# Swin block and convolution block over 16 images: the front of image n+2 made in the feed-forward stretch of image n+1

## The reference

```
t    = layernorm(tok)                                  # tok: 1024 tokens x 128, in 16 windows of 64
q, k, v = t @ qkv_w.T + qkv_b                          # 8 heads of 16
a    = softmax(q k^T / 4 + bias) v                     # in each window
tok  = tok + a @ proj_w.T + proj_b
tok  = tok + gelu(layernorm(tok) @ w1.T + b1) @ w2.T + b2     # 128 -> 512 -> 128

out0 = gelu(conv1x1(x));  x_att, adaptive = from the mean of out0
x_fca = |x_att| * |out0|                               # what abs(ifft2(fft2(out0) * x_att)) gives
x_sca = fgm(conv1x1(mean x_fca) * x_fca)               # fft2, high frequencies boosted, abs(ifft2)
h, v = 1x7 and 7x1 dilated, then 3x3, all depthwise;   pyr = four dilated 3x3 grouped, then 3x3
edge = sigmoid(conv3x3(out0)); cw = softmax(base * adaptive)
out  = conv1x1(relu(x + cw0 (1+edge) h + cw1 (1+edge) v + cw2 (1-.3 edge) pyr + cw3 point + cw4 x_sca))
```

## Time and profile before

| | us |
|---|---|
| runs shown: lowest, median, highest of 3 | 1802.71, 1813.92, 1819.46 |
| the profiled execution: its own time | 1805.41 |
| its span, first to last instruction | 1803.6 |
| from one `rectify` to the next, 15 cycles apart in all | 106.57 to 109.88 |

### The profile page before, as it was taken

One profiled execution on the slowest core, in us unless ns is written; L12 is line 12 of the kernel. 1 busy time (PEld: TensorE's weight loads), 2 busy tenths in 40 slices (PEclk: granted clock), 3 DMA queues, 4 the chain that ended last, 5 costly groups with the idle time before them and its releaser, 6 DMA issues.

```text
span 1803.6 us, 32142 instructions
## 1 busy us (share of the span) xinstructions
PE 1549.4 (86%) x11664; PEld 906.3 (50%) x11664; DVE 1364.0 (76%) x2455; ACT 864.2 (48%) x1380; POOL 684.9 (38%) x603
## 2 busy tenths in 40 slices
PE   5789899888989889888998988889888898988884
PEld 3346455464555546445463554546455464555542
DVE  4558778687777878788687777868788786778866
ACT  2344545455454544545455454544545545454533
POOL 3244251634416244251534416134251623416151
PEclk9899999999999999999999999999999999999997
DMA  4011020111102011020111102011020201102020
GB/s 147 1 26 41 26 52 1 43 33 37 39 23 53 0 37 39 25 51 0 43 33 37 39 23 53 0 37 39 25 51 0 58 18 37 39 12 53 0 54 12
DMA packets 19618, 60.23 MB, mean 33 GB/s; under 512 B 6228, under 2 KB 6228, under 8 KB 19204
## 3 DMA queue, kind: packets, MB, share of 16 engines
q1 hardware_dynamic: 19588, 59.83, 13.7%
HBM read 14.04 MB, written 9.02 MB: 13 GB/s over the span
## 4 chain that ended last, share of the span: by engine, by line
DVE 39%; PE 25%; DVEq 16%; issue 7%; ACT 6%; SPq 4%; DMA 3%; ACTq 1%; POOL 0%; POOLq 0%
DVE hv L1090 16%; DVEq L959 7%; DVE nT L929 5%; PE bank L647 5%; PE bank L674 4%; SPq L428 4%; DVE row_max L960 4%; DVEq L965 3%; PE bank L467 3%; PE bank L518 3%; PE bank L489 2%; DMA k_heads<-kC 2%; PE bank L755 2%; DVE score L957 2%; PE bank L577 1%
## 5 line engine op out<-in xcount | busy, mean ns | idle before, releaser
L674 PE MATMUL bank<-act,mats_sb 128*32 128x512 f32 (+11 forms) x2112 | 267.1, 475 | 1.4 <-DVE xs L1026 1.4
L1666 POOL TENSOR_TENSOR score<-score,row_max 128x512 f32<-128x512 f32 x128 | 133.4, 1042 | 306.7 <-DVE row_max L960 305.1
L1350 ACT ACTIVATE fft<-bank 128x512 f32<-128x512 f32 x224 | 168.9, 807 | 125.7 <-PE bank L467 111.8
L1090 DVE SCALAR_TENSOR_TENSOR hv<-hor,mix,hv 128x1024 f32<-128x1024 f32 x128 | 193.8, 1514 | 10.7
L467 PE MATMUL bank<-cons_sb,fft 128*128 128x128 f32 x1280 | 185.4, 306 | 11.8 <-DVE fft L1117 11.8
L1090 DVE SCALAR_TENSOR_TENSOR hv<-ver,mix,hv 128x1024 f32<-128x1024 f32 x144 | 186.9, 1298 | 11.0
L1382 ACT ACTIVATE score<-score 128x512 f32<-128x512 f32 x128 | 80.8, 631 | 225.8 <-POOL score L1666 225.8
L467 PEld LDWEIGHTS bank<-cons_sb,fft 128*128 128x128 f32 x1280 | 172.7, 217 | 31.4 <-DVE fft L1117 17.0
L1677 POOL COPY inv_wide<-row_inv 128x128 f32<-128x128 f32 x128 | 91.8, 717 | 206.7 <-DVE row_inv L966 206.7
L674 PEld LDWEIGHTS bank<-act,mats_sb 128*32 128x32 f32 x2112 | 117.5, 109 | 99.6 <-issue 81.5
L1696 POOL TENSOR_SCALAR hor<-act,cols_sb 128x1024 f32<-128x1024 f32 x16 | 18.0, 1125 | 391.6 <-ACT act L1407 391.6
(11 more groups left out here) (180 smaller groups left out, 2903.9 us busy)
## 6 DMA issues: line engine op xcount, KB each, us to landing
pyr_stack<-pyr SPq DMA_DIRECT2D x192, 144.2 KB, 3.1
x_in<-x_dram SPq DMA_DIRECT2D x16, 512.0 KB, 3.5
k_heads<-kC SPq DMA_DIRECT2D x128, 64.0 KB, 2.4
out_dram<-y_out SPq DMA_DIRECT2D x16, 512.0 KB, 2.8
k_heads<-rel_dram SPq DMA_DIRECT2D x2, 1024.0 KB, 13.0
mats_sb<-mats_dram SPq DMA_DIRECT2D x1, 1978.5 KB, 7.4
z_dram<-z_sb SPq DMA_DIRECT2D x32, 19.1 KB
z_run<-z_dram SPq DMA_DIRECT2D x16, 38.2 KB
```

What stands on the lines that cost most here:

```text
L674: last = pe.matmul(grids[32 * d:32 * d + 32, y0 - 16 * k:y1 - 16 * k, x0:x1], w_pyr[:, d, t], act[:, y0 + dy:y1 + dy, x0 + dx:x1 + dx], st ...
L1090: last = dve.scalar_tensor_tensor(hv[:], src, mix[:, a, k:k + 1], hv[:], ALU.mult, ALU.add)
L1350: return act_.activation(dst, src, ACT.Copy)
L1666: pool.tensor_tensor(score[:, j % 3], score[:, j % 3], row_max[:, j % 3].unsqueeze(2).broadcast_to([P, HEADS, WT]), ALU.subtract)\
```

## The change

The first steps of the Swin block, from the tokens to queries, keys and values (its *front*), leave the front of the cycle and go one cycle earlier. `both(n, i, f)` now has three images in work: the convolution block of n, attention and feed-forward of i = n+1, and the front of f = n+2. The last cycle has f = None. `swin_rest(0, 1)` makes the front of image 1 too, and the front of image 0 is made before it.

- The next image's token transposes go through bank 3 in slots 6 and 7 (`next_turns`), `norm1_stats(f)` after slot 7, `norm1(f)` after the fourteenth tap, and its n transposes, keys, queries and values between the up and down products of `mlp`, in banks 4 to 7, which the convolution block has emptied by then.
- New tiles: `attn_out` has its own memory (and holds nC1, the transposed first normalisation), `xT` shares memory with `qC`, `x1T` has its own, statistics of the two normalisations are apart.
- Waits: `in_conv` waits for the queries of the front (bank 4, 5), `gap_products`, `edge_products` and `out_conv` for its values (bank 6, 7), `spread_inverse(i, 1)` for `x_copy(f)` (bank 3).
- `SLOT_TAPS` goes from 9 to 13 taps in the slots. The second half of the pyramid, of which 5 of 9 steps stood ahead of slot 0, now lies wholly in slots 0 and 1, and its waits for `route_z` and `xs_sb` are gone. `conv_early` stands before `scores(i, j+2)`. `r_even_bias` stands before slot 3's taps.
- SP issues `spread_keys(n+2)` and `load(n+3)` behind `stack_pyramid(n)`.

```diff
-        attn_out = xw
-        xT = sb("xT", CH, C)
-        x1T = xT
+        attn_out = sb("attn_out", TOK)
+        nC1 = attn_out
+        x1T = sb("x1T", CH, C)
+        xT = qC.rearrange("p (c d) -> p c d", c=CH)
...
-        SLOT_TAPS = (0, 0, 0, 2, 4, 4, 5, 7, 9)
+        SLOT_TAPS = (0, 0, 0, 2, 4, 6, 7, 10, 13)
...
+            with sp.Fori(0, IMAGES - 3) as n:
                 spread_edge(n)
-                spread_keys(n + 1)
                 stack_pyramid(n)
+                load(n + 3)
+                spread_keys(n + 2)
                 store(n)
...
-            def mlp(i):
+            def mlp(i, n=None, f=None):
...
+                def value(k):
+                    pe.wait_ge(k_sb, 2 * f + k + 1)
+                    v(f, k, 6 + k)
                 for t in range(3):
-                    up(t)
+                    up(i, t)
                 n2_transposes(i, 1)
-                for t in range(3, 6):
-                    up(t)
-                down(0)
-                up(6)
-                up(7)
-                down(1)
+                up(i, 3)
+                up(i, 4)
+                half_of(turn, 0)
+                up(i, 5)
+                half_of(turn, 1)
+                down(i, 0)
+                half_of(key, 0)
+                half_of(key, 1)
+                up(i, 6)
+                half_of(query, 0)
+                half_of(query, 1)
+                up(i, 7)
+                half_of(value, 0)
+                half_of(value, 1)
+                down(i, 1)
...
+            def next_turns(i, f, k):
+                if k == 0:
+                    pe.wait_ge(s_biased, 8 * i + 8)
+                else:
+                    pe.wait_ge(xT_sb, 2 * f + 1)
+                x_transposes(f, k, 3)
...
             # PE
-            def both(n, i):
-                in_conv(n)
-                x_transposes(i)
+            def both(n, i, f):
+                scores(i, 0)
+                in_conv(n, i + 1)
+                scores(i, 1)
                 edge_products(n)
                 pyramid(n, 0, range(0, 2))
                 gap_products(n)
-                pyramid(n, 0, range(2, 7))
-                n_transposes(i)
+                pyramid(n, 0, range(2, 6))
                 mid_products(n)
-                queries_keys(i)
-                v(i)
-                pyramid(n, 0, range(7, 9))
-                scores(i, 0)
-                scores(i, 1)
-                pyramid(n, 1, range(0, 5))
+                pyramid(n, 0, range(6, 9))
                 for j in range(PAIRS):
+                    conv_early(n, j)
                     if j + 2 < PAIRS:
                         scores(i, j + 2)
-                    conv_early(n, j)
                     prob_transposes(i, j)
...
                     conv_late(n, j)
+                    if f is not None and j >= 6:
+                        next_turns(i, f, j - 6)
...
             # DVE
-            def both(n, i):
+            def both(n, i, f):
+                bias_max(i, 0)
                 gap(n)
-                norm1_stats(i)
+                bias_max(i, 1)
                 attention_vectors(n)
-                norm1(i)
-                keys(i)
                 scaled_input(n)
                 even_part(n)
-                bias_max(i, 0)
                 route_logits(n)
-                bias_max(i, 1)
                 for j in range(PAIRS):
...
+                if f is not None:
+                    norm1_stats(f)
                 residual_stats(i, 0)
                 scale_values(i, 1)
                 norm2(i, 0)
                 residual_stats(i, 1)
                 norm2(i, 1)
-                taps(n, range(SLOT_TAPS[PAIRS], 18))
+                taps(n, range(SLOT_TAPS[PAIRS], 14))
+                if f is not None:
+                    norm1(f)
+                taps(n, range(14, 18))
+                if f is not None:
+                    keys(f, (6, 7))
                 gate_axes(n)
...
             # ACT, in mlp_gelu(i, f) behind the gelu of up product t
+                        if t in (4, 5):
+                            n_copy(f, t - 4, t)
+                        elif t == 6:
+                            queries(f, 0, 4)
+                            queries(f, 1, 5)
+                        elif t == 7:
+                            v_copy(f, 0, 6)
+                            v_copy(f, 1, 7)
...
             # ACT
-            def both(n, i):
-                to_windows(i)
+            def both(n, i, f):
                 in_gelu(n)
-                x_copy(i)
                 magnitudes(n)
                 edge_products_copy(n)
-                deviation1(i)
-                n_copy(i)
-                queries(i)
+                exponent(i, 0)
                 route_tanh(n)
-                v_copy(i)
-                exponent(i, 0)
                 route_exponent(n)
                 exponent(i, 1)
...
             # POOL
-            def both(n, i):
-                axis_conv(n, 0, OFFSETS)
+            def both(n, i, f):
+                less_max(i, 0)
+                axis_conv(n, 0, OFFSETS[:2])
+                less_max(i, 1)
+                axis_conv(n, 0, OFFSETS[2:])
                 axis_conv(n, 1, OFFSETS[:3])
-                residual_in(i)
-                less_max(i, 0)
-                less_max(i, 1)
...
                 square_sum(n)
+                if f is not None:
+                    residual_in(f)
```

More of the change, by code:

```diff
@@ L486, in queries_keys @@
[L486 to L495, removed]
@@ L497, in v @@
-            def v(i):
-                wv = w_qkv[:, 2 * C:3 * C].rearrange("p (g e d) -> p e g d", g=HP, e=2)
[L499 to L506, removed]
+                turn4(bank[b], xw, k).then_inc(xT_ps, 1)
@@ new lines, in down @@
+            def down(i, k):
+                b = (0, 3)[k]
+                pe.wait_ge(up_sb, 8 * i + 4 + 4 * k)
+                for c in range(4):
+                    pe.matmul(bank[b][:, c * P:(c + 1) * P], x1T[:, 4 * k + c], ident, is_transpose=True,
+                              start=(c == 0), stop=False)
+                for f in range(FC):
+                    last = pe.matmul(bank[b][:], w_down[:, f * P:(f + 1) * P],
+                                     hidden[:, f, HALF * k:HALF * k + HALF], start=False, stop=(f == FC - 1))
+                last.then_inc(down_ps, 1)
@@ L901, in _ @@
             pe.wait_ge(setup_dve, 1)
-            swin_rest(0)
-            both(0, 1)
-            with pe.Fori(1, IMAGES - 1) as n:
-                both(n, n + 1)
+            for k in range(2):
+                key_products(0, k, 2 + k)
+            for k in range(2):
+                query_products(0, k, k)
+            for k in range(2):
+                pe.wait_ge(q_sb, k + 1)
+                v(0, k, k)
+            swin_rest(0, 1)
+            both(0, 1, 2)
+            with pe.Fori(1, IMAGES - 2) as n:
+                both(n, n + 1, n + 2)
+            both(IMAGES - 2, IMAGES - 1, None)
             conv_only(IMAGES - 1)
@@ L1309, in _ @@
             dve.sem_inc(setup_dve, 1)
-            swin_rest(0)
-            both(0, 1)
-            with dve.Fori(1, IMAGES - 1) as n:
-                both(n, n + 1)
+            keys(0, (2, 3))
+            swin_rest(0, 1)
+            both(0, 1, 2)
+            with dve.Fori(1, IMAGES - 2) as n:
+                both(n, n + 1, n + 2)
+            both(IMAGES - 2, IMAGES - 1, None)
             conv_only(IMAGES - 1)
@@ L1623, in _ @@
             to_windows(0)
-            x_copy(0)
+            for k in range(2):
+                x_copy(0, k, k)
             deviation1(0)
-            n_copy(0)
+            for k in range(2):
+                n_copy(0, k, 2 + k)
             act_.wait_ge(setup_dve, 1)
             act_.wait_ge(zeroed, 1)
-            swin_rest(0)
-            both(0, 1)
-            with act_.Fori(1, IMAGES - 1) as n:
-                both(n, n + 1)
+            for k in range(2):
+                queries(0, k, k)
+            for k in range(2):
+                v_copy(0, k, k)
+            swin_rest(0, 1)
+            both(0, 1, 2)
+            with act_.Fori(1, IMAGES - 2) as n:
+                both(n, n + 1, n + 2)
+            both(IMAGES - 2, IMAGES - 1, None)
             conv_only(IMAGES - 1)
```

255 lines of the change are left out of this document (139 added, 116 removed).

## The result

The changed kernel takes 1978.4 us (median of 4 runs, 1974.5 to 1982.4) against 1814.9: a ratio of 1.091, 95% interval 1.086 to 1.096. It is slower by 164 us, four times the 40 that I forecast, and outside the range of 1785 to 1893. The profiled execution took 1981.9, its span is 1980.1 us.

What follows compares the result with a forecast made beforehand. It took the bound as mixed by stretch: a chain through all engines in front, DVE in slots, PE and DVE in the tail. -13.9 + 5.3 + 3.4 + 7.9 = +2.7 a cycle, together +40: 1855 us, range 1785 to 1893.

Steps and rivals of the forecast that it cites:

- forecast 13.9: Front of the cycle, from both act halves ready to DVE's slot 0: 13.9 us instead of 27.8, so -13.9.
- 38.4 forecast: Tail, from the end of DVE's slot 7 to the next cycle's act: 38.4 us instead of 30.5.
- 109.4: Whole cycle: 71.0 us to the end of the slots plus 38.4 of tail, against 106.7, +2.7 a cycle.
- 4.0 forecast: even_part on DVE ahead of slot 0: 4.0 us, the middle of 2.4 to 5.4.
- its own range: Range of the main forecast from bounds of even_part and the slots' waits: 1820 to 1890 us.
- a rival on the faster side alone: PE keeps the full clock once the DMA wait goes: at most 85 us back, 1770 us; chance 0.22.
- wait for DVE in slots 4 and 5 longer than now: PE's longer waits ahead of inverse_even, named as evidence against the rising clock; no size given.
- POOL's axis taps: POOL work beside even_part at the front's end, considered in setting even_part's 4.0 us.
- My term of +3.4: Slots: DVE waits for PE's scores, +3.4 us a cycle, bounds nothing to 5.
- Slot 2, forecast at 5.2: DVE's slot 2: 5.2 us in the walk, against 4.7 before.
- the +5.3: Slots on DVE: four more taps at 1.33 us, two in slot 4 and two behind gate_pyramid, +5.3 a cycle.
- its +7.9: Tail: new PE products and later statistics, less filled waits and moved to_windows, +7.9 us a cycle.

Runs made afterwards that it cites:

- e1_fill: The changed kernel with nine extra matmuls a cycle, results unread, in three of PE's waits; 1886.4 us, ratio 1.040 to the kernel before.
- e11_pool_fill: e1_fill with POOL's second axis convolution spread over slots 0 to 3; 1822.5 us, ratio 1.005 to the kernel before.
- e4_taps: The changed kernel with the taps spread as before the change, 9 of 18 in the slots instead of 13; 1979.6 us, ratio 1.092 to before.
- e9_fill_taps: e1_fill with 9 of 18 taps in the slots instead of 13; 1918.8 us, ratio 1.057 to the kernel before.
- e6_scores: The changed kernel with POOL's second axis convolution spread, norm1_stats behind norm2(i, 0), and scores ahead of conv_early; 1782.9 us, ratio 0.983 to before.
- e7_all_fill: e6_scores with six extra matmuls a cycle, two in each of three PE waits; 1758.4 us, ratio 0.969 to the kernel before.

## Why the prediction was wrong

**The direction and the frame were right.** The front of the cycle shrinks from 27.8 to 12.8 us (forecast 13.9), the keys' DMAs drop off the path, and the tail grows because PE has the new products where it had no idle time: 38.9 us at full clock against 38.4 forecast. The stretches of e1_fill, whose tail is at full clock and whose slots are nearly so, add up to 112.3 against 109.4. `even_part` came at 3.4 us (4.0 forecast): its first operation took 2.9 us, but its 30-column one 0.2, where it had taken 2.4 beside `residual_in`. The recorded sums have two slips that change nothing: 1805.4 + 40 is 1845 and not 1846, and 3 us a cycle under the forecast make 1813 for the lower end of its own range and not 1820.

**The step that failed is the clock.** The prediction walked every operation of PE in the new order at the duration that it had before, which puts the cost of a lower clock at nothing, and kept the clock for a rival on the faster side alone, with the argument that the DMA wait would go. The granted clock did the opposite, 0.953 to 0.871. It even named the fact that speaks against it, that PE would "wait for DVE in slots 4 and 5 longer than now", and gave that no price. The waits came, 3.8 and 2.8 us, and a third that my own walk implied: `norm1_stats` and `residual_stats(0)` ahead of `scale_values(1)` leave PE without work between `last_odd` and `project(1)` for over 4 us. I had counted there only when `mlp` starts. The three waits were 1.0, 1.0 and 0.15 us before. Filling them gives back 92 us, where the forecast missed by 123. It is the largest term, and not the only one.

**POOL's queue was left out.** I walked PE, DVE and ACT and costed "POOL's axis taps" only as neighbours of `even_part`. With the front 15 us shorter, `less_max(2)` is wanted 15 us earlier, but the axis convolution ahead of it starts at A as ever and holds POOL until 19 us after it. Price with the waits filled: 4.5 us a cycle (64 us).

My term of +3.4 for DVE waiting for PE came out in slots 0 and 1 by luck alone (14.3 as forecast). DVE waits for no scores there. The slots are 3 us longer because DVE's own operations take longer while POOL's axis convolution runs beside them, first in the kernel before and then after:

```profile
1004.03 2.27 DVE L1131 SCALAR_TENSOR_TENSOR xm<-xs,mix,xm 128x1024 f32<-128x1024 f32 x1
...
1010.49 0.30 DVE L1034 TENSOR_TENSOR fft<-xs 128x30 f32<-128x30 f32 x1
```

```profile
974.31 3.03 DVE L1170 SCALAR_TENSOR_TENSOR xm<-xs,mix,xm 128x1024 f32<-128x1024 f32 x1
...
981.14 1.53 DVE L1073 TENSOR_TENSOR fft<-xs 128x30 f32<-128x30 f32 x1
```

The 30-column operation ends at 982.67, 0.07 us behind POOL's of 2.99 us shown above, in agreement with the rule that the prediction weighed, of the Trainium skill ("SBUF — State Buffer", "SBUF: two separate sides"), that the loser of the lock on the shared port pair waits for the whole instruction of the other. With POOL's work spread (e11_pool_fill) the waits for the scores that I had forecast do come, 0.2 and 1.0 us, and the two slots take 13.3. Slot 2, forecast at 5.2, took 8.5, and 4.8 to 5.2 with POOL's work spread: what was missing there is POOL's queue.

**The order of the scores was under-priced.** In slot 5 I took no wait for `scores(7)` behind `edge_spread`; slot 4 came out at 8.0 instead of 6.5 with the waits filled. The order's effect is 4.6 us a cycle with the clock's share and about 2.5 without; slot 4, to which I had given nothing for it, has most of it.

**The taps were charged for nothing.** Of the +5.3 the half behind `gate_pyramid` came as forecast (11.5 instead of 8.7). The half in slot 4 goes into DVE's wait for the scores: the slot takes 8.9 us with these two taps and 9.7 without them. And I let the tail give nothing back, since DVE had slack there. DVE has it only behind `norm1`: ahead of it each tap delays PE's turn. In all the four taps cost 0 in the kernel as it was (after, e4_taps) and -2.3 a cycle with the waits filled (e1_fill, e9_fill_taps).

These terms have both signs and partly cancel, so that the kernel with the clock and POOL mended (1822.5) comes under the 1855 forecast, for partly wrong reasons: the nearness is luck.

What stays open: how the three waits share the 92 us was not tried one by one, what a clock held up everywhere would give is not shown, and no run takes the new products out of the tail, so that its +7.9 is shown by the timelines alone.

## What to carry to other kernels

Before you walk a new order at old durations, look for every place where PE will stand still longer than before, and price the work behind it at the lower clock, from rows that show it there; here filling the waits gave back 92 of 164 us. When a stretch is shortened, list for every engine what stands in its queue ahead of the first thing that the next stretch wants: work that used to be hidden (POOL's convolution) does not shrink along. A change that loses can hold a gain: the same loop turned, with POOL's work spread, the statistics later and the scores first, is 1.7% faster than before, and 3.1% with PE kept busy.

## What the runs showed that I had not expected

Useless matmuls made four kernels faster: nine a cycle by 92 us and, with POOL's work spread, by 63, six by 24, five in the kernel before by 16. The cycles of the kernel after are all alike, 119.4 to 119.5 us but for the first and the last, and the edit of the taps, which moved 3 us from one stretch to another, left them at 119.5 too; those of e6_scores are alike too (105.8 to 106.0). Those of the kernel before vary from 106.6 to 109.9, those of e1_fill from 111.3 to 115.6 and those of e7_all_fill from 103.4 to 106.2. So one cycle's timeline is not the kernel's mean in these, and a saving read from a single cycle can be off by 1 us or more. No run here explains why some kernels vary and others don't.
